# A graph, attention and mixture-of-experts layer: where the groups without edges stand, how the sorted places are loaded, and routed writes without a bound

## The chip, the cores and the metric

One of the cores of a Trainium2 chip runs the whole program in one launch. The metric is the device time of one execution in microseconds (us). The engines are PE (TensorE), DVE (VectorE), ACT (ScalarE), POOL (GpSimd) and SP (SyncE); the last two also issue transfers.

## The reference

```python
xn = _layernorm(x)                                   # x: 6250 x 256, 100000 edges (src, dst)
# graph attention over the edges, rows = src, neighbours = dst
e = leaky(f_dst_part[dst] + f_row_part[src] + a_b)   # slope 0.2
ex = exp(e - segment_max(e, src)[src])
h = relu(segment_sum(ex / denom[src] * Wh[dst], src))
# linear attention with 8 heads and a feed-forward block on xn, each with a layernorm
x = x + h + mix(xn)
# 6 experts of three 256x256 layers, the best two of each row by a router
x = x + moe(_layernorm(x))
```

## The kernel before

The 6250 nodes are 50 blocks (NT) of R = 125 rows. **Sorting.** The edges come sorted by dst and are needed by src, so the kernel sorts them on the chip: DVE and PE turn 28 chunks of edges into places, and POOL writes each chunk's words to `sorted_slots` in HBM (L524). An edge's place is in one of TILES = 812 tiles of L = 128; the tiles of a block follow those of the block before, and two blocks can share one. While the sorting runs, the linear attention is worked off between its steps in numbered slots (`attend`).

**The group table.** The graph loop takes the edges in groups of GT = 4 tiles, each of one block. How many groups a block needs depends on the data (`ngf`, from its first and last tile), but the loop has a fixed number, NG = 251, enough for any input. So DVE computes, from the counts, a word per group: its first tile `tf`, its place in the ring and its block (`group_tab`, one row of 251 words). Before the change the groups that are left over stand behind the last block's: `over` is held at block NT - 1 and `tf` at TILES - 4. To go from 50 blocks to 251 groups, PE multiplies 0/1 comparisons (`gcmp`) with a column per block. A second row of the table says, for each of NB = 203 ring places, how many groups must be done before the place is filled anew.

**Sorted places.** When the last chunk is written (`sent_runs`), SP loads the 812 x 128 words back as `raw`, in seven transfers of up to 128 tiles; PE transposes them (L1218) and DVE makes of them the index table of the gathers and the row table (L894 to L900). Then a barrier ends the block of code.

**The graph loop.** POOL gathers rows of `wh_table` (1036 bytes each) by an indirect transfer per tile (L1306) into a ring of RING = 11 places of four tiles, and waits for `room` before it fills a place again. SP watches what landed and counts `ready`; it also waits, for the place two ahead, until PE's `total` has freed it, and copies three tiles at each turn of the ring. Each group passes fixed stages, one slot apart, on all engines: `own_rows` on ACT (L1495), which waits for `ready` and is the first to touch a group; `mark` on DVE (four of L1340); `turn` on PE one slot later; peak, `spread`, `fetch`; the scores at lag 4; `own_weight` and `weigh` at lag 5; `total` on PE at lag 6 (L1607, L1619); `gather_up` on DVE at lag 7 (L1409), which adds the group into its block's row of `acc_mem`. In every ten slots one of the 25 chunks of the feed-forward block is worked off as well. `acc_mem`, 128 x 12900, lies over the sorting's tables (`raw` among them) and has to be zero before the first `gather_up`; one memset at the loop's start does that (L1315).

**Routing and experts.** The router works in five parts of 6, 10, 10, 12 and 12 tiles of rows. As soon as a part's places are known (`d_pos`, L1904) POOL writes every row twice, 125 rows of 264 words per indirect transfer (L1809): 12, 20, 20, 24 and 24 of them. Each has a bound, `bounds_check=last_row`. When all have landed the expert stage reads the rows back in tiles of 256, PE multiplies them three times, and POOL adds the results to the output (L2110).

## Time and profile before

| | |
|---|---|
| median of 3 runs | 2435.78 us (2430.62 to 2439.38) |
| the profiled execution | 2439.61 us |
| its span, first to last instruction | 2437.9 us |
| busy: PE, DVE, ACT, POOL | 1952.8, 1758.0, 1440.8, 1129.3 us |
| mean granted clock of PE | 0.915 of full speed |

Busy times are sums over stages that have different limits, so no share of the span says which engine matters; each stage is read by itself. A source view gives for one line of the code how often it ran, the least, median and greatest length of one in ns, and when the first and the last started. A bracket behind a row of the timeline tells how long the engine had been idle before it and whose event ended that; "issue" is time in which it waited for nothing that the profile shows.

### The profile page before, as it was taken

Reading aid. Unit: us, or ns where it says so; the run is one execution under the profiler, and the core shown is the slowest. Engines: PE = TensorE matmul, PEld = TensorE weight load, DVE = VectorE, ACT = ScalarE, POOL = GpSimd, SP = SyncE. Lnnn points to the kernel's source line nnn. Section 1 sums busy time; section 2 is a strip of 40 time slices with the busy share of each in tenths; the row PEclk is TensorE's granted clock in tenths of the full one; section 3 lists DMA queues with packets and bytes.
Section 4 is the critical chain, followed back from the end, with each engine's and each line's share of the span. In section 5 each row is a group of like instructions: output and inputs, shape, how many; then the busy total and the mean of one; then the engine's idle time right before and its main releaser. Section 6 shows DMA issues by size and latency. Waiting matters only on the chain. (4 is left out here: it accounts for less than half of the span.)

```text
span 2437.9 us, 50376 instructions
## 1 busy us (share of the span) xinstructions
PE 1952.8 (80%) x10273; PEld 1581.1 (65%) x10273; DVE 1758.0 (72%) x5447; ACT 1440.8 (59%) x4447; POOL 1129.3 (46%) x1089
## 2 busy tenths in 40 slices
PE   2888856598874888988889998998799564399997
PEld 1444435477762777767677877777678463288886
DVE  7877769999984778787768888887788752155543
ACT  3566547233311778877778888887688762133332
POOL 0000000011125777777777777777720177455555
PEclk9899967799986999999999999999999875699998
DMA  4200000011112444444444444444410455255553
GB/s 136 59 26 27 28 2 22 13 55 23 24 21 76 121 118 116 122 124 117 121 117 118 121 117 121 117 116 121 124 41 6 123 141 139 75 88 92 94 97 57
DMA packets 123284, 205.68 MB, mean 84 GB/s; under 512 B 34806, under 2 KB 77667, under 8 KB 122987
## 3 DMA queue, kind: packets, MB, share of 16 engines
q0 software_dynamic: 69648, 135.12, 23.8%
q1 hardware_dynamic: 48681, 59.88, 8.3%
q10 hardware_dynamic: 4658, 7.46, 1.1%
q8 instruction: 96, 1.57, 0.3%
q14 instruction: 201, 1.65, 0.2%
HBM read 146.67 MB, written 49.70 MB: 81 GB/s over the span
## 5 line engine op out<-in xcount | busy, mean ns | idle before, releaser
L1306 POOL DMA_INDIRECT area<-wh_table,area x812 | 783.8, 965 | 260.1 <-issue 246.4
L1619 PE MATMUL bank<-area 128*126 x2008 | 512.4, 399 | 103.8 <-ACT area L1542 70.1
L1619 PEld LDWEIGHTS bank<-area 128*126 128x126 f32 x2008 | 366.6, 192 | 186.8 <-issue 134.0
L1340 DVE TENSOR_SCALAR area<-iota_row,area 128x126 f32<-128x126 f32 x1004 | 357.9, 364 | 33.1 <-ACT area L1495 27.5
L1528 ACT ACTIVATE area<-iota_row,area 128x126 f32<-128x126 f32 x753 | 292.4, 389 | 0.4 <-ACT area L1535 0.3
L1409 DVE SCALAR_TENSOR_TENSOR acc_mem<-acc_mem,area,bank 125x258 f32 x251 | 120.7, 481 | 179.6 <-PE bank L1607 168.1
L1542 ACT ACTIVATE area<-area 128x126 f32<-128x126 f32 x753 | 243.1, 387 | 0.5
L2110 POOL DMA_INDIRECT out_dram<-area x108 | 169.2, 1567 | 158.7 <-DVE area L2171 142.3
L519 POOL IOTA acc_mem<- 50x812 f32 x1 | 0.8, 807 | 457.7 <-DVE area L789 457.7
L1481 ACT ACTIVATE area<-bank 125x512 bf16<-125x512 f32 x251 | 148.7, 592 | 95.8 <-DVE area L1350 94.0
L1639 PE MATMUL bank<-area 128*128 128x250 f32 x800 | 191.0, 382 | 4.0 <-ACT area L1555 4.0
L1650 PE MATMUL bank<-area 128*125 128x256 f32 x800 | 193.3, 385 | 0.0
L1595 PE MATMUL bank<-ident,area 128*126 128x128 f32 x1004 | 161.7, 284 | 35.3 <-DVE area L1340 34.9
L1639 PEld LDWEIGHTS bank<-area 128*128 128x128 f32 x800 | 156.3, 196 | 25.0 <-ACT area L1555 4.5
L1350 DVE TENSOR_REDUCE area<-bank 125x1 f32<-125x512 f32 x251 | 171.6, 684 | 0.0
L1650 PEld LDWEIGHTS bank<-area 128*125 128x125 f32 x800 | 153.7, 192 | 24.7
L1495 ACT ACTIVATE area<-area,iota_blk 128x4 f32 x251 | 74.5, 297 | 140.0 <-SPq L1298 122.7
L524 POOL DMA_INDIRECT sorted_slots<-area x28 | 46.0, 1645 | 230.4 <-DVE area L868 209.3
L2171 DVE SCALAR_TENSOR_TENSOR area<-bank,area 128x256 f32<-128x256 f32 x108 | 47.6, 480 | 144.2 <-DMA out_dram<-area 81.9
L1809 POOL DMA_INDIRECT moe_rows<-area x100 | 120.9, 1209 | 63.3 <-ACT area L1960 33.8
L1595 PEld LDWEIGHTS bank<-ident,area 128*126 128x126 f32 x1004 | 106.4, 141 | 39.8 <-DVE area L1340 39.4
L2203 ACT ACTIVATE area<-bank,area 128x256 f32<-128x256 f32 x108 | 45.3, 471 | 139.8 <-issue 133.6
(395 smaller groups left out, 4217.1 us busy)
## 6 DMA issues: line engine op xcount, KB each, us to landing
area<-moe_rows SPq DMA_DIRECT2D x54, 264.0 KB, 2.7
area<-wh_table,area POOLq DMA_INDIRECT x812
area<-area SPq DMA_DIRECT2D x18, 388.5 KB, 3.4
wh_table<-area SPq DMA_DIRECT2D x50, 126.5 KB
xn<-in_x_dram SPq DMA_DIRECT2D x25, 250.0 KB
x_rows<-area SPq DMA_DIRECT2D x25, 250.0 KB
area<-x_rows ACTq DMA_DIRECT2D x24, 250.0 KB
area<-in_L_ffn_expert_w_dram SPq DMA_DIRECT2D x3, 1536.0 KB, 12.1
```

The lines of the kernel that those rows point to most:

```text
L1306: g.indirect_dma_start(out=gath[:, (i + GT) % RS, :], out_offset=None, in_=table, in_offset=bass.IndirectOffsetOnAxis(ap=idx_tab[:, i:i + ...
L1340: ins = V.tensor_scalar(xm[:, b, t, :], iota_row[:, :], rowl[:, j % 10, t:t + 1], fetched(j, D)[:, t:t + 1], ALU.is_equal, ALU.mult)
L1350: V.tensor_reduce(gmax[0:R, b:b + 1], bank[XT[j % 2]][0:R, :], AX.X, ALU.max).then_inc(d_m, 1)
L1481: A.activation(hot[0:R, b, :], bank[XT[j % 2]][0:R, :], ACT.Sign).then_inc(a_hot, 1)
L1528: last = A.activation(dist[:, t, :], iota_row[:, :], ACT.Abs, bias=rowl[:, j % 10, t:t + 1], scale=-1.0)
L1542: last = A.activation(sm[:, b, t, :], dist[:, t, :], ACT.Exp, bias=e3[:, b, t:t + 1], scale=-1.0e12)
L1595: last = T.transpose(bank[XT[j % 2]][0:RW, t * L:(t + 1) * L], xm[:, b, t, :], ident[:, :])
L1619: last = T.matmul(bank[US[b]][0:RW, 0:WROW], sm[:, b, t, :], gath[:, bass.ds(place + t, 1), 0:WROW].rearrange("p a w -> p (a w)"), start=( ...
L1639: last = T.matmul(bank[HB[p % 2]][:, i * CH:(i + 1) * CH], w_1[:, k, f * 128:(f + 1) * 128], x1T[:, k, :], start=(k == 0), stop=(k == 1))
L1650: last = T.matmul(bank[AB][0:R, r * D:(r + 1) * D], hT[:, f, r * R:(r + 1) * R], w_2[:, f, :], start=(f == 0), stop=(f == 7))
L1809: g_.indirect_dma_start(out=moe_rows, out_offset=bass.IndirectOffsetOnAxis(ap=posi3[0:R, b, k, i:i + 1], axis=0), in_=pay3[0:R, b, i, :], ...
L2110: g.indirect_dma_start(out=out, out_offset=bass.IndirectOffsetOnAxis(ap=rowi[:, j % RB6, s, MW - 2:MW - 1], axis=0), in_=yo[:, j % 3, s, : ...
```

## The change

Three edits. First, the left-over groups are shared out: after block b, `sparef` = (b + 1) x left / 50 + 0.25 as an integer have been laid, and each belongs to an extra block 50, whose rows in `acc_mem`, `own_mem` and `fr_c` nobody reads, and begins at the tile that the next block's first group begins with. Two comparisons are needed (`gcmp`, `gspare`), four matmuls of 251 columns, and a turn of `tf` by PE for the second row of the table. The memset of `acc_mem` is split: the columns that the sorting doesn't use (5360) are cleared ahead of the wait for the transposes, the others (7798) by `clear`, lag 3, in the loop's fourth slot. Second, `raw` is loaded by two transfers. Third, L1809 has no bound.

```diff
-        own_mem = sb("own_mem", [R, NT * 3 * (1 + OLD)])
+        own_mem = sb("own_mem", [R, (NT + 1) * 3 * (1 + OLD)])
-        acc_mem = sb("acc_mem", [128, NT * WROW])
-        acc = acc_mem[0:R, :].rearrange("p (b w) -> p b w", w=WROW)
+        acc_mem = sb("acc_mem", [128, (NT + 1) * WROW])
+        acc_all = acc_mem[0:R, :].rearrange("p (b w) -> p b w", w=WROW)
+        acc = acc_all[:, 0:NT, :]
...
                 sp.wait_ge(sent_runs, 16 * KC)
-                for i in range(-(-TILES // 128)):
-                    n = min(128, TILES - i * 128)
-                    sp.dma_start(raw[0:n, i, :], slots[i * 128 * L:(i * 128 + n) * L].rearrange("(t l) -> t l", l=L)).then_inc(slots_in, 16)
+                full = TILES // 128
+                sp.dma_start(raw[:, 0:full, :], slots[0:full * 128 * L].rearrange("(i t l) -> t i l", t=128, l=L)).then_inc(slots_in, 16)
+                sp.dma_start(raw[0:TILES - full * 128, full, :],
+                             slots[full * 128 * L:TILES * L].rearrange("(t l) -> t l", l=L)).then_inc(slots_in, 16)
...
                 step(V.tensor_copy(ngf, int50))
+                V.tensor_tensor(packed[:, 3, :], firstf[:, 1:NT + 1], firstf[:, 0:NT], ALU.subtract)
                 step(V.tensor_tensor_scan(gend, ones[:, 0:NT], ngf, 0.0, ALU.mult, ALU.add))
...
+                V.tensor_copy(packed[:, 5, :], tmp50)
+                step(V.tensor_scalar(left, gend[:, NT - 1:NT], -1.0, float(NG), ALU.mult, ALU.add))
+                V.tensor_copy(packed[:, 4, :], firstf[:, 1:NT + 1])
+                step(V.tensor_scalar(lastf, iota_g[:, 1:NT + 1], left, 1.0 / NT, ALU.mult, ALU.mult))
+                step(V.tensor_scalar(int50, lastf, 0.25, None, ALU.add))
+                step(V.tensor_copy(sparef[:, 1:NT + 1], int50))
+                V.tensor_tensor(packed[:, 0, :], gend, sparef[:, 1:NT + 1], ALU.add)
+                step(V.tensor_tensor(ngf, ngf, sparef[:, 1:NT + 1], ALU.add))
+                V.tensor_tensor(packed[:, 1, :], gend, sparef[:, 0:NT], ALU.add)
+                step(V.tensor_tensor(packed[:, 2, :], ngf, sparef[:, 0:NT], ALU.subtract))
+                step(V.tensor_tensor(packed, packed, ident[:, 0:NT].unsqueeze(1).to_broadcast([128, 6, NT]), ALU.mult))
+                step(V.tensor_reduce(cols, packed, AX.X, ALU.add))
+                V.tensor_scalar(gspare, iota_g[0:NT, :], rcol[0:NT, :], None, ALU.is_ge)
                 V.tensor_scalar(gcmp, iota_g[0:NT, :], gcol[0:NT, :], None, ALU.is_ge).then_inc(gcmp_ready, 1)
...
                 dve.wait_ge(gmap_done, 1)
-                step(V.scalar_tensor_tensor(tf, iota_g, float(GT), bank[KV][:, 128:128 + NG], ALU.mult, ALU.add))
-                V.tensor_scalar(over, bank[KV + 1][0:1, 128:128 + NG], float(NT - 1), None, ALU.min)
...
+                begun, ended = bank[KV][0:1, 0:NG], bank[KV + 1][0:1, 0:NG]
+                groups, past = bank[KV][0:1, 256:256 + NG], bank[KV + 1][0:1, 256:256 + NG]
+                step(V.tensor_copy(whole, ended))
+                V.tensor_tensor(shown, iota_g[0:1, :], groups, ALU.subtract)
+                step(V.tensor_tensor(spot, past, whole, ALU.subtract))
+                V.tensor_scalar(over, whole, -1.0, float(NT), ALU.mult, ALU.add)
+                step(V.scalar_tensor_tensor(shown, spot, -1.0, shown, ALU.add, ALU.mult))
+                V.tensor_tensor(over, spot, over, ALU.mult)
+                step(V.scalar_tensor_tensor(tf, shown, -float(GT), begun, ALU.mult, ALU.add))
+                V.tensor_tensor(over, over, whole, ALU.add)
+                V.tensor_scalar(tf, tf, float(TILES - GT), None, ALU.min).then_inc(gcmp_ready, 1)
+                dve.wait_ge(gcmp_ready, 2)
...
+                dve.wait_ge(gmap_done, 2)
+                V.tensor_scalar(tq0, bank[KV][:, 508:509], -3.0, 1.0 / GT, ALU.add, ALU.mult)
...
+                V.memset(acc_mem[:, ZERO_FROM:], 0.0)
                 dve.wait_ge(tab_pe, 1)
...
-                T.matmul(bank[KV][:, 128:128 + NG], more[0:NT, :], gcmp, start=True, stop=True)
-                T.matmul(bank[KV + 1][:, 400:401], gcmp[:, 0:L], wcol[0:NT, :], start=True, stop=True)
-                T.matmul(bank[KV + 1][0:NG - L, 401:402], gcmp[:, L:NG], wcol[0:NT, :], start=True, stop=True)
-                T.matmul(bank[KV + 1][:, 128:128 + NG], ones[0:NT, :], gcmp, start=True, stop=True).then_inc(gmap_done, 1)
+                T.matmul(bank[KV][0:1, 0:NG], dcolf[0:NT, :], gspare, start=True, stop=True)
+                T.matmul(bank[KV][0:1, 256:256 + NG], scol[0:NT, :], gcmp, start=True, stop=True)
+                T.matmul(bank[KV + 1][0:1, 0:NG], ones[0:NT, 0:1], gcmp, start=True, stop=True)
+                T.matmul(bank[KV + 1][0:1, 256:256 + NG], ones[0:NT, 0:1], gspare, start=True, stop=True).then_inc(gmap_done, 1)
+                pe.wait_ge(gcmp_ready, 2)
+                T.matmul(bank[KV][:, 508:509], tf[:, 0:L], ones[0:1, 0:1], start=True, stop=True)
+                T.matmul(bank[KV][0:NG - L, 509:510], tf[:, L:NG], ones[0:1, 0:1], start=True, stop=True).then_inc(gmap_done, 1)
...
-                V.memset(acc_mem[:, :], 0.0).then_inc(acc_zero, 1)
-                dve.wait_ge(acc_zero, 3)
+                dve.wait_ge(acc_zero, 2)
...
+                def clear(s, j):
+                    if at(s) == 0:
+                        V.memset(acc_mem[:, 0:ZERO_FROM], 0.0).then_inc(acc_zero, 1)
...
-                               (4, score_less_max)], feed)
+                               (4, score_less_max), (3, clear)], feed)
...
                             g_.indirect_dma_start(out=moe_rows, out_offset=bass.IndirectOffsetOnAxis(ap=posi3[0:R, b, k, i:i + 1], axis=0),
-                                                  in_=pay3[0:R, b, i, :], in_offset=None,
-                                                  bounds_check=last_row, oob_is_err=False).then_inc(sent[b], 16)
+                                                  in_=pay3[0:R, b, i, :], in_offset=None).then_inc(sent[b], 16)
```

The order of the instructions, in two places. On DVE, where the group table is made (`bank` is PSUM; 1x251 is one row over the groups). Before:

```order
L822 SCALAR_TENSOR_TENSOR acc_mem<-area,bank 128x251 [waits gmap_done]
L823 TENSOR_SCALAR acc_mem<-bank 1x251 [waits rank_step]
L824 SCALAR_TENSOR_TENSOR acc_mem<-area,bank 128x1
L825 SCALAR_TENSOR_TENSOR acc_mem<-area,bank 123x1
L826 TENSOR_SCALAR acc_mem<-acc_mem 128x251
L827 TENSOR_SCALAR acc_mem<-acc_mem 128x1 [waits rank_step]
L828 TENSOR_SCALAR acc_mem<-acc_mem 123x1
L829 SCALAR_TENSOR_TENSOR acc_mem<-acc_mem 1x251
L830 TENSOR_SCALAR acc_mem<-acc_mem 128x1 [waits rank_step]
```

and in the change, behind the same wait for PE:

```order
L837 COPY acc_mem<-bank 1x251 [waits gmap_done]
L838 TENSOR_TENSOR acc_mem<-area,bank 1x251 [waits rank_step]
L839 TENSOR_TENSOR acc_mem<-bank,acc_mem 1x251
L840 TENSOR_SCALAR acc_mem<-acc_mem 1x251 [waits rank_step]
L841 SCALAR_TENSOR_TENSOR acc_mem<-acc_mem 1x251
L842 TENSOR_TENSOR acc_mem<-acc_mem 1x251 [waits rank_step]
L843 SCALAR_TENSOR_TENSOR acc_mem<-acc_mem,bank 1x251
L844 TENSOR_TENSOR acc_mem<-acc_mem 1x251 [waits rank_step]
L845 TENSOR_SCALAR acc_mem<-acc_mem 1x251
L847 SCALAR_TENSOR_TENSOR acc_mem<-acc_mem 1x251 [waits gcmp_ready]
L848 TENSOR_SCALAR acc_mem<-acc_mem 1x251 [waits rank_step]
```

Operations on single columns (128x1, 123x1) gave way to ones on rows of 251, and the second wait for PE stands further down, ahead of the comparisons for the ring. On DVE, at the end of the sorting, behind the last `join` (L868 before, L887 now). Before:

```order
L868 SCALAR_TENSOR_TENSOR area<-area,bank 106x64 [waits sent_runs,halved] x2
L894 CAST acc_mem<-bank 128x512 [waits tab_pe]
L894 CAST acc_mem<-bank 128x300
L896 TENSOR_SCALAR area<-acc_mem 128x812 [waits rank_step]
L897 TENSOR_SCALAR acc_mem<-acc_mem 128x812
```

and in the change:

```order
L887 SCALAR_TENSOR_TENSOR area<-area,bank 106x64 [waits sent_runs,halved] x2
L910 MEMSET acc_mem 128x5360
L914 CAST acc_mem<-bank 128x512 [waits tab_pe]
L914 CAST acc_mem<-bank 128x300
L916 TENSOR_SCALAR area<-acc_mem 128x812 [waits rank_step]
```

A memset of 5360 columns now stands ahead of the wait for `tab_pe`, the transposes. On DVE, in the graph loop, between the last two marks of group 3 (ISA rows fetch a register) and the next slot, which begins with `group_peak`. Before:

```order
L1331 ISA
L1340 TENSOR_SCALAR area<-iota_row,area 128x126
L1331 ISA
L1340 TENSOR_SCALAR area<-iota_row,area 128x126
L1350 TENSOR_REDUCE area<-bank 125x1 [waits p_xt]
L1262 TENSOR_LOAD group_tab
```

and in the change:

```order
L1353 ISA
L1362 TENSOR_SCALAR area<-iota_row,area 128x126
L1353 ISA
L1362 TENSOR_SCALAR area<-iota_row,area 128x126
L1371 MEMSET acc_mem 128x7798
L1376 TENSOR_REDUCE area<-bank 125x1 [waits p_xt]
L1285 TENSOR_LOAD group_tab
```

The memset that stood at the loop's start (L1315, 12900 columns) is gone from there, and 7798 columns of it stand here.

## Rows read from the trace of the kernel before

**Rows 1.** Windows: us, busy us (count) of each engine, clock, DMA.

```profile
core 0: us, PE busy (x) PEld busy (x) DVE busy (x) ACT busy (x) POOL busy (x), PEclk, DMA share, GB/s
...
480.00:733.00 253.00, 215.85 (x1424) 190.66 (x1424) 231.16 (x376) 74.67 (x197) 42.95 (x26) 0.92 0.13 29
...
754.80:1787.50 1032.70, 896.39 (x5053) 744.62 (x5054) 808.61 (x3133) 802.95 (x2897) 783.80 (x812) 0.96 0.43 119
1787.50:1893.00 105.50, 100.17 (x589) 83.92 (x587) 87.79 (x350) 92.80 (x334) 0.00 (x0) 1.00 0.02 7
```

**Rows 2.** Source view of the gathers, L1306 (ns; first and last start us).

```profile
L1306 POOL DMA_INDIRECT area<-wh_table,area x812: 949/949/1543, 754.9 to 1785.1; - x163
```

**Rows 3.** Source view of own_rows, L1495, one per group; what ended idleness.

```profile
L1495 ACT ACTIVATE area<-area,iota_blk x251: 282/297/302, 761.6 to 1891.8; 128x4 f32 x126
...
  SPq L1298: 122.7, 61
```

**Rows 4.** The same line, window 1278 to 1474 us.

```profile
L1495 ACT ACTIVATE area<-area,iota_blk x48: 291/298/300, 1278.6 to 1473.0; 128x4 f32 x48
```

**Rows 5.** The same line, window 1787.5 to 1893 us.

```profile
L1495 ACT ACTIVATE area<-area,iota_blk x26: 291/297/298, 1788.0 to 1891.8; 128x4 f32 x26
```

**Rows 6.** Source view of gather_up, L1409, one per group.

```profile
L1409 DVE SCALAR_TENSOR_TENSOR acc_mem<-acc_mem,area,bank x251: 467/483/485, 798.7 to 1914.1; 125x258 f32 x126
```

**Rows 7.** Timeline, POOL: start us, length us, line; near 815 us.

```profile
815.27 0.95 POOL L1306 DMA_INDIRECT area<-wh_table,area  x1 [0.30 <-issue]
```

**Rows 8.** Timeline, DVE, start of the graph stage.

```profile
757.28 10.81 DVE L1315 MEMSET acc_mem<- 128x12900 f32 x1 [2.62 <-issue]
```

**Rows 9.** Timeline, DVE, where the group table is made.

```profile
467.24 0.26 DVE L803 TENSOR_TENSOR_SCAN acc_mem<-ones,acc_mem 128x50 f32<-128x50 f32 x1
...
470.09 0.25 DVE L817 TENSOR_TENSOR own_mem<-own_mem 125x50 f32<-125x50 f32 x1
...
472.85 0.42 DVE L822 SCALAR_TENSOR_TENSOR acc_mem<-area,bank 128x251 f32<-128x251 f32 x1 [0.36 <-PE bank L1197]
...
479.34 0.64 DVE L872 MEMSET area<- 128x308 uint32 x2
```

**Rows 10.** Timeline, PE, the first of the four matmuls for it.

```profile
469.93 1.20 PE L1194 MATMUL bank<-area 50*128 50x251 f32 x2 [5.68 <-DVE area L815]
```

**Rows 11.** Timeline, SP, PE weight load and DVE, 744 to 751 us.

```profile
744.31 3.14 SPq L476 DMA_DIRECT2D acc_mem<-sorted_slots  x7
748.79 1.14 PEld L1218 LDWEIGHTS bank<-ident,acc_mem 128*128 128x128 f32 x6 [10.69 <-DMA acc_mem<-sorted_slots]
...
750.64 1.07 DVE L894 CAST acc_mem<-bank 128x512 int32<-128x512 f32 x2 [17.57 <-PE bank L1218]
```

**Rows 12.** The page, DMA issues: KB each, us from issue to landing.

```profile
area<-area SPq DMA_DIRECT2D x18, 388.5 KB, 3.4
```

**Rows 13.** Source view of the routed writes, L1809.

```profile
L1809 POOL DMA_INDIRECT moe_rows<-area x100: 1185/1194/1623, 1942.9 to 2100.6; - x100
```

**Rows 14.** Timeline, POOL, at the starts of the second and fourth bursts.

```profile
1968.35 1.34 POOL L1809 DMA_INDIRECT moe_rows<-area  x1 [7.06 <-ACT area L1960]
...
2029.91 1.21 POOL L1809 DMA_INDIRECT moe_rows<-area  x1 [0.30 <-POOL area L1802]
```

**Rows 15.** Timeline, DVE, L1904, which lets bursts three and four start.

```profile
1991.36 0.18 DVE L1904 CAST area<-area 125x20 int32<-125x20 f32 x1
...
2020.41 0.18 DVE L1904 CAST area<-area 125x24 int32<-125x24 f32 x1
```

**Rows 16.** Source view of the sorting writes, L524.

```profile
L524 POOL DMA_INDIRECT sorted_slots<-area x28: 1547/1550/3732, 507.9 to 740.6; - x28
```

**Rows 17.** Source view of the output writes, L2110.

```profile
L2110 POOL DMA_INDIRECT out_dram<-area x108: 1544/1554/1774, 2129.8 to 2428.1; - x108
```

**Rows 18.** The page, part 5, one kind of VectorE instruction.

```profile
L1340 DVE TENSOR_SCALAR area<-iota_row,area 128x126 f32<-128x126 f32 x1004 | 357.9, 364 | 33.1 <-ACT area L1495 27.5
```

More of the change, by code:

```diff
@@ L248, in gps_kernel @@
         iota_g, gcmp = take(NG), take(NG)[0:NT, :]
-        more = take(128)
         rstd_all, nmr = (take(NT)[0:R] for _ in range(2))
@@ L322, in gps_kernel @@
         int50, end50 = (a.bitcast(I32) for a in smallt[7:9])
-        firstf = take(NT + 1)
-        gcol, csrc, tcol, wcol, pcol, tq0, tq1 = (take(1) for _ in range(7))
+        firstf, sparef = take(NT + 1), take(NT + 1)
+        csrc, left, tq0, tq1 = (take(1) for _ in range(4))
+        cols = take(6)
+        gcol, rcol, scol, dcolf, tcol, pcol = (cols[:, i:i + 1] for i in range(6))
         srci, dsti = wpos.bitcast(I32), bpos.bitcast(I32)
@@ L335, in gps_kernel @@
         behind = take(L)[0:NT, :]
-        tf = take(NG)
+        tf = take(NG)[0:1, :]
         spot, whole, over = (take(NG)[0:1, :] for _ in range(3))
@@ L340, in gps_kernel @@
         rcmp = take(2, NB)
+        gspare = take(NG)[0:NT, :]
+        shown = take(NG)[0:1, :]
+        packed = take(6, NT)
+        ZERO_FROM = take.place[0]
         XB, QB, HEADS, NUM, DEN, OUT = 0, 1, 2, 3, 4, 5
@@ L801, in _ @@
                 V.memset(firstf[:, NT:NT + 1], float(TILES))
+                V.memset(sparef[:, 0:1], 0.0)
                 step(V.tensor_copy(ngf, int50))
+                V.tensor_tensor(packed[:, 3, :], firstf[:, 1:NT + 1], firstf[:, 0:NT], ALU.subtract)
                 step(V.tensor_tensor_scan(gend, ones[:, 0:NT], ngf, 0.0, ALU.mult, ALU.add))
-                step(V.scalar_tensor_tensor(ngf, ngf, -float(GT), firstf[:, 1:NT + 1], ALU.mult, ALU.add))
-                V.tensor_tensor(tmp50, tmp50, ident[:, 0:NT], ALU.mult)
@@ L813, in _ @@
-                step(V.tensor_reduce(gcol, tmp50, AX.X, ALU.add))
-                V.tensor_scalar(more[0:NT, :], ones[0:NT, :], wcol[0:NT, :], None, ALU.mult)
-                V.tensor_scalar(gcmp, iota_g[0:NT, :], gcol[0:NT, :], None, ALU.is_ge).then_inc(gcmp_ready, 1)
-                step(V.tensor_scalar(own_all[:, :, 0, 0], frd, csrc[0:R, :], None, ALU.add))
-                step(V.tensor_tensor(own_all[:, :, 0, 1], own_all[:, :, 0, 0], own_bits[:, :, 0, 0], ALU.subtract))
-                V.tensor_tensor(own_all[:, :, 0, 2], own_all[:, :, 0, 1], own_bits[:, :, 0, 1], ALU.subtract)
@@ new lines, in _ @@
+                step(V.tensor_reduce(cols, packed, AX.X, ALU.add))
+                V.tensor_scalar(gspare, iota_g[0:NT, :], rcol[0:NT, :], None, ALU.is_ge)
+                V.tensor_scalar(gcmp, iota_g[0:NT, :], gcol[0:NT, :], None, ALU.is_ge).then_inc(gcmp_ready, 1)
+                V.memset(own_all[:, NT:NT + 1, 0, :], 0.0)
+                V.memset(fr_c[:, NT:NT + 1], 0.0)
+                step(V.tensor_scalar(own_all[:, 0:NT, 0, 0], frd, csrc[0:R, :], None, ALU.add))
+                step(V.tensor_tensor(own_all[:, 0:NT, 0, 1], own_all[:, 0:NT, 0, 0], own_bits[:, 0:NT, 0, 0], ALU.subtract))
@@ L829, in _ @@
-                step(V.scalar_tensor_tensor(word, over, 65536.0, tf[0:1, :], ALU.mult, ALU.add))
-                V.tensor_scalar(tq0, tq0, 1.0 / GT, None, ALU.mult)
-                step(V.tensor_scalar(tq1[0:NG - L, :], tq1[0:NG - L, :], -3.0, 1.0 / GT, ALU.add, ALU.mult))
-                V.tensor_scalar(rcmp[:, 0, :], iota_g[:, 0:NB], tq0, None, ALU.is_ge)
-                V.tensor_scalar(rcmp[0:NG - L, 1, :], iota_g[0:NG - L, 0:NB], tq1[0:NG - L, :], None, ALU.is_ge).then_inc(gcmp_ready, 1)
@@ L834, in _ @@
-                step(V.tensor_scalar(spot, tf[0:1, :], float(GT), None, ALU.add))
+                begun, ended = bank[KV][0:1, 0:NG], bank[KV + 1][0:1, 0:NG]
[4 more added lines that the diff above has]
+                V.tensor_scalar(over, whole, -1.0, float(NT), ALU.mult, ALU.add)
@@ new lines, in _ @@
+                step(V.scalar_tensor_tensor(shown, spot, -1.0, shown, ALU.add, ALU.mult))
[4 more added lines that the diff above has]
+                dve.wait_ge(gcmp_ready, 2)
+                step(V.scalar_tensor_tensor(word, over, 65536.0, tf, ALU.mult, ALU.add))
@@ L835, in _ @@
+                step(V.tensor_scalar(spot, tf, float(GT), None, ALU.add))
                 step(V.tensor_scalar(turns, spot, 0.5, 1.0 / RS, ALU.add, ALU.mult))
@@ L883, in _ @@
                     if k == 2:
[L884 removed]
+                        dve.wait_ge(gmap_done, 3)
                         dve.wait_ge(halved, 1)
@@ L1233, in gps_kernel @@
         pair = take(GT, 2)
-        peak = take(NT)
+        peak = take(NT + 1)
         e1, e2, e3 = (take(2, GT) for _ in range(3))
@@ L1322, in block_of @@
                 def block_of(j):
-                    return dve.snap(blocks[j % 10], min_val=0, max_val=NT - 1)
+                    return dve.snap(blocks[j % 10], min_val=0, max_val=NT)
                 def load_place(s, j):
@@ L1497, in block_of @@
                 def block_of(j):
-                    return act.snap(blocks[j % 5], min_val=0, max_val=NT - 1)
+                    return act.snap(blocks[j % 5], min_val=0, max_val=NT)
                 def rescale(s, j):
@@ L1602, in fetch @@
                     wait(pe, d_es, at(s, 3, -5))
-                    r = pe.snap(blocks[b], min_val=0, max_val=NT - 1)
+                    r = pe.snap(blocks[b], min_val=0, max_val=NT)
                     g = 1 + at(s) % OLD
```

40 lines of the change are left out of this document (16 added, 24 removed).

## Prediction, made before the changed kernel was run

> **What bounds the kernel now.** The windows view gives the stages [rows 1]. From 754.8 to 1787.5 us all five engines work at the graph loop: POOL gathers 812 tiles of 128 table rows, and PE, DVE and ACT work them off in groups of four. From 1787.5 to 1893 POOL is idle and the others go on at full pace. The source view of the gathers says why: first start 754.9, last 1785.1 [rows 2], so 1030.2/811 = 1.270 us per gather and 5.08 per ring place of four. Busy is 0.949 of it; with the bare issue gap a gather costs 1.25, so the queue never pauses for long. On the other side stands `own_rows`, once per group, from 761.6 to 1891.8, and 122.7 us of ACT's idle time before it ended with SP's word that tiles have landed, in 61 places [rows 3]. So the loop is bound by gathers until 1787 and by the group pipeline after it.
>
> What a group costs when nothing is missing is read from two stretches: (1473.0 - 1278.6)/47 = 4.136 us while gathers run [rows 4] and (1891.8 - 1788.0)/25 = 4.152 after they ended [rows 5]. They agree, so the gathers don't slow the engines; I take 4.15. The 25 groups behind the last gather are the kernel's empty ones. Counting the reference's edge list by the kernel's rule gives blocks of 4 (24 of them) or 5 (26) groups, 226 with edges, of 251. Before, the 226 are paced by the gathers, though 1030/4.15 = 248 would fit, and then the 25 are paid alone: 104 us with POOL idle.
>
> The second POOL-bound stretch is the routing: 100 writes of L1809 [rows 13], the second burst starting at 1968.35 [rows 14] and the last write at 2100.6, at 1.50 us each. Then nothing else is left of that stage, and the expert stage, bound by PE, can't start before they land.
>
> **Part 1, empty groups between the blocks.** Half a group per block is laid behind it; none is left at the end. The engines then need 251 x 4.15 = 1042 us for what POOL feeds in 1030: engines and gathers are level, the engines a little behind. The start is still fed by POOL. Group 13, counted from 0, reads tiles 47 to 50, in ring place 12; that place's first gather starts at 815.27 [rows 7], its fourth 3.8 later, and from there to `own_rows` takes 2.9 (1785.1 to 1788.0) [rows 2, 5]: 822.0. From there 237 groups x 4.15 = 983.6, so the last `own_rows` stands at 1805.6. I add 4 us for places where groups still wait, such as the ring wrap. 1809.6 against 1891.8 [rows 3]: **-82**. What follows it stays: the last `gather_up` comes 22 us later [rows 6].
>
> Bounds: it can't end before its tiles, 1788.0, which is -104. Above: a ring place is freed when `total` of its groups is done. At the start `own_rows` to `gather_up` takes 798.7 - 761.6 = 37 us [rows 3, 6], at the end 22; call it 32 with full feed. 11 places are 56 us of gathers, less 32, less 7 for gather and landing: 17 us, four groups, that the engines may fall behind before POOL is held. The longest run of 5-group blocks has nine; with half an empty group each takes 22.8 us and feeds on 16.1 tiles, 20.5: +2.3 a block, +21 in the run. So POOL is held some 4 to 10 us there, while the engines stay busy; in a run of 4-group blocks they catch up and may wait for the tiles that came late. If each held us is lost and other runs add as much, -62. I keep -82.
>
> The table that places them costs DVE more. Before, from the scan to L817 are 14 steps in 2.85 us [rows 9], 0.20 each; now 19 steps, two of them on 300 columns (+0.25 each): +1.5. PE multiplies four times 251 columns instead of twice; a pair of passes takes 1.20 [rows 10], two small ones go: +1.2 of waiting for DVE. From L822 to L872 DVE took 6.5 us [rows 9]; six more operations of one row by 251, some 0.33, four single columns of 0.1 less: +1.6. Together **+4**. It isn't hidden: DVE is busy 231 of the 253 us behind it [rows 1], and each step of the sorting waits for it. Bounds +2 (half swallowed by the waits there) and +6. The new second wait, for `tf` turned by PE, stands behind seven operations of DVE and costs nothing; PE holds its `inverses` for it by some 4 us, of which DVE wants the result 10 us later.
>
> The clearing of `acc_mem` was one memset of 10.81 us at 757.28 [rows 8]. Now 5360 columns (4.5 us at that rate) lie in DVE's wait of 17.57 us for the transposes [rows 11]: nothing. The other 7798 (6.5 us) stand in slot 3 of the loop, near 777 us, where a group comes only each 5.02 us. Up to group 13 DVE has 45 us for ten groups, and a group costs it 87.8/25 = 3.5 us [rows 1]: 35 + 6.5 fit, so nothing; at worst 3, if all engines need 4.15 (41.5 + 6.5). While the old memset ran, gathers went on at 1.25 us. The Trainium skill, page "SBUF — State Buffer", section "SBUF: two separate sides", says that a VectorE operation in a two-port mode locks GpSimd out, so that its DMAs lack descriptors. By that rule, were a memset such an operation, the 6.5 us would be added to the gathers and the total be 2342 to 2343; the row speaks against it.
>
> **Part 2, two transfers for seven.** SP's seven issues take 3.14 us from 744.31, PE starts at 748.79, 4.5 behind the first [rows 11]. A transfer of 388.5 KB, nearly the new one's 384, lands 3.4 us after its issue [rows 12]: 747.7, with the small one and PE's start 748. **-1**; bounds 0 and -2.
>
> **Part 3, writes without a bound.** Two kinds of rows bear on it. The gathers have no bound and take 0.949 + 0.303 = 1.252 [rows 2]; the routed writes, with one, 1.194 + 0.303 = 1.497 [rows 13]. If the difference is the bound, each saves 0.245. But the sorting writes (106 rows of 64) have none either and take 1.55 [rows 16], as the output writes with bound and addition do [rows 17]: shape and direction count as well. The gather is nearest in width (259 and 264 columns, 128 and 125 rows), so I take 0.245; ends are 0 and +0.36 more per write. The second burst starts with DVE, so 88 writes are on the path: -21.6. Bursts two and three end 40 x 0.245 = 9.8 earlier than 2029.91 [rows 14], at 2020.1, and burst four needs L1904 of 2020.41 [rows 15]: 0.7 is lost. **-21**.
>
> **Sum.** The profiled execution took 2439.6 us (span 2437.9 and 1.7 around it), 3.8 over the median. 2439.6 + 4 - 1 - 82 - 21 = 2339.6; less 3.8: **2336**.
>
> **Rivals.** A, as above, 0.50. B, the bound costs nothing and the 0.245 is the scatter's or the 125 rows': 2336 + 21 = 2357; speaks for it that the sorting writes are dear without one; 0.22. C, the bare writes cost like those, 1.55: 88 x 0.36 = 32 more than before, 2389; 0.05. D, POOL and engines hold each other by turns, -62: 2356; for it speaks that both sides are within 2% of each other with 17 us between them; 0.12. E, DVE locks POOL: if each of the 25 added groups' five operations of 0.364 [rows 18] stopped the gathers for its length, 45 us, the gathers end at 1834 instead of 1788 and own 250 with them, some 26 above my 1809.6: 2362. That is the port rule named above as a mechanism here; the mean step of 5.08 against the bare 5.01 leaves 14 us for all such stops in 226 groups, 1.6 for 25 more; 0.03. F, the empty groups stay at the end because of how the shares are rounded: 2439.6 + 3 - 21 - 3.8 = 2418; the shares come in steps of half a group, so little speaks for it; 0.03. G, slower: the empty groups close the ring on itself. A place's way round (gather and landing 7, own to total 32, release some 2, and up to two empty groups more, 8) is 49 us for 11 places of 5.08, 56. Beyond 56 the loop goes by the way, not by the engines, and since the loop takes 1137 us now (754.9 to 1891.8) and the other parts give 18, it passes the old time from (1137 + 18)/203 x 11 = 63 us. If it were 66, 203 x 6 = 1218, 81 over: 2336 + 82 + 81 = 2499; 0.03.
>
> Range: A alone 2323 to 2348. With B, D and most of E 2318 to 2368, leaving C, F, G and the tails out. A measurement here tells some 0.3% (7 us) from no change. Faster holds A to F, 0.95; slower G and the worst of C, 0.03; same 0.02.
>
> **What would show it.** `own_rows` without a long stretch behind the last gather: last gather near 1795, last `own_rows` near 1813 (with the +3), steps of 4.15 throughout, ACT's waits for SP below 30 us; POOL's waits for room some 5 to 25 us where before they were 0.9. If the step in the loop is above 4.3, or both waits stand at 40 us, the -82 is wrong. L1904's copies at the same distances, L1809's successor with a median of 0.95; at 1.19 B holds, at 1.55 C. The first gather at 758; PE's transposes 3.7 behind SP's first issue. DVE from the scan to the first one-hot 4 us longer.

## The result, and the profile after

The changed kernel took 2350.3 us (median of 4, 2348.6 to 2353.0), the kernel before in the same session 2436.8; the ratio is 0.965, 95% interval 0.963 to 0.967. So 86.5 us were won, where 100 were forecast. Executions in a slower state are left out of a ratio, so it can differ a little from the quotient of the two medians.

The windows view of the kernel after, with the columns of [rows 1]:

```profile
core 0: us, PE busy (x) PEld busy (x) DVE busy (x) ACT busy (x) POOL busy (x), PEclk, DMA share, GB/s
480.00:731.00 251.00, 213.38 (x1426) 188.72 (x1427) 231.52 (x377) 74.69 (x197) 42.83 (x26) 0.94 0.13 30
750.80:1791.00 1040.20, 962.53 (x5581) 805.35 (x5582) 882.36 (x3452) 892.87 (x3202) 782.61 (x811) 0.98 0.43 118
1791.00:1800.00 9.00, 9.00 (x56) 7.61 (x55) 7.01 (x31) 7.20 (x27) 0.95 (x1) 1.00 0.12 32
```

The stretch of 105 us in which POOL had nothing left [rows 1] is 9 us now. The stretch before it is only 7.5 us longer, and DVE and ACT do 319 and 305 more instructions in it: the empty groups' work. The source views of the gathers, of `own_rows` and of `gather_up`, as in [rows 2, 3, 6]:

```profile
L1329 POOL DMA_INDIRECT area<-wh_table,area x812: 945/947/1519, 750.8 to 1791.1; - x163
its engine sat idle before it (us, times) until:
  issue: 241.6, 793
  SPq L1316: 16.0, 18
```

```profile
L1523 ACT ACTIVATE area<-area,iota_blk x251: 283/297/301, 758.4 to 1799.5; 128x4 f32 x126
its engine sat idle before it (us, times) until:
  SPq L1321: 27.7, 9
```

```profile
L1437 DVE SCALAR_TENSOR_TENSOR acc_mem<-acc_mem,area,bank x251: 466/482/485, 793.7 to 1821.8; 125x258 f32 x126
```

First to last `own_rows` is 1041.1 us; before it was 1130.2 [rows 3]. ACT waits for tiles in 9 places instead of 61, and 22.9 of the 27.7 us stand before the first five groups, where the gathers have only begun. POOL now waits for room in the ring (SP's L1316) in 18. The timeline of POOL between 1395 and 1450 us, its rows that ended such a wait:

```profile
1398.99 0.94 POOL L1329 DMA_INDIRECT area<-wh_table,area  x1 [4.86 <-SPq L1316]
...
1420.12 0.94 POOL L1329 DMA_INDIRECT area<-wh_table,area  x1 [1.11 <-SPq L1316]
...
1444.91 0.94 POOL L1329 DMA_INDIRECT area<-wh_table,area  x1 [4.46 <-SPq L1316]
```

They fall where the engines are at the end of the run of nine blocks with five groups each and just behind it, 10.4 of the 16.0 us. The source view of the routed writes, to be set against [rows 13], shows the part that failed:

```profile
L1836 POOL DMA_INDIRECT moe_rows<-area x100: 1174/1180/1500, 1852.0 to 2009.3; - x100
```

A median of 1.180 us without the bound, 1.194 with it; first to last write 157.3 us, before 157.7. The timeline of POOL, SP, PE's weight load and DVE between the sorting and the loop, beside [rows 8, 11]:

```profile
737.23 1.54 POOL L531 DMA_INDIRECT sorted_slots<-area  x1 [3.61 <-DMA sorted_slots<-area]
...
740.95 0.38 SPq L481 DMA_DIRECT2D acc_mem<-sorted_slots  x1
...
741.38 0.48 SPq L482 DMA_DIRECT2D acc_mem<-sorted_slots  x1
...
744.69 1.15 PEld L1241 LDWEIGHTS bank<-ident,acc_mem 128*128 128x128 f32 x6 [10.30 <-DMA acc_mem<-sorted_slots]
...
746.54 1.07 DVE L914 CAST acc_mem<-bank 128x512 int32<-128x512 f32 x2 [11.58 <-PE bank L1241]
...
750.78 1.00 POOL L1329 DMA_INDIRECT area<-wh_table,area  x1 [12.01 <-POOLq L449]
```

The transposes stand 3.74 us behind SP's first issue (before 4.48). The part of the memset that moved into the loop, in DVE's timeline:

```profile
776.66 6.56 DVE L1371 MEMSET acc_mem<- 128x7798 f32 x1 [1.57 <-PE bank L1623]
```

DVE's row of the new table, from the scan on (before: [rows 9]):

```profile
463.59 0.25 DVE L812 TENSOR_TENSOR_SCAN acc_mem<-ones,acc_mem 128x50 f32<-128x50 f32 x1
...
467.57 0.25 DVE L830 TENSOR_TENSOR own_mem<-own_mem 125x50 f32<-125x50 f32 x1
...
470.93 0.41 DVE L837 COPY acc_mem<-bank 1x251 f32<-1x251 f32 x1 [0.95 <-PE bank L1217]
...
476.90 0.41 DVE L854 SCALAR_TENSOR_TENSOR group_tab<-acc_mem 1x251 int32<-1x251 f32 x1
```

### The profile page after: what moved, and what is told of

It is laid out like the page before. It is cut to its first block and busy times, and to the rows that moved or that the text cites. A ratio compares the mean times of both kernels' runs of the same rounds, so it can differ in the third digit from the quotient of the medians.

```text
span 2346.8 us, 50388 instructions
## 1 busy us (share of the span) xinstructions
PE 1927.8 (82%) x10277; PEld 1565.0 (67%) x10277; DVE 1758.4 (75%) x5456; ACT 1446.5 (62%) x4447; POOL 1128.2 (48%) x1089
## 5 line engine op out<-in xcount | busy, mean ns | idle before, releaser
L1647 PE MATMUL bank<-area 128*126 x2008 | 497.5, 390 | 34.4 <-ACT area L1570 15.7
L1647 PEld LDWEIGHTS bank<-area 128*126 128x126 f32 x2008 | 358.6, 188 | 110.1 <-issue 58.4
L1678 PEld LDWEIGHTS bank<-area 128*125 128x125 f32 x800 | 150.1, 188 | 22.9
L1205 PE MATMUL bank<-area 128*128 128x128 f16 x784 | 104.6, 298 | 7.5 <-DVE area L887 7.5
```

What stands on the lines that cost most here:

```text
L1647: last = T.matmul(bank[US[b]][0:RW, 0:WROW], sm[:, b, t, :], gath[:, bass.ds(place + t, 1), 0:WROW].rearrange("p a w -> p (a w)"), start=( ...
L1678: last = T.matmul(bank[AB][0:R, r * D:(r + 1) * D], hT[:, f, r * R:(r + 1) * R], w_2[:, f, :], start=(f == 0), stop=(f == 7))
```

## The experiments

The first four kernels shared a chip with runs of the kernel before (2435.2 us there, median of 19).

**e1_nobound**: the kernel before, with the bound alone taken from the routed writes.

```diff
-                last_row = g_.to_reg(ROWS - 1)
...
-                                                   in_=pay3[0:R, b, i, :], in_offset=None,
-                                                   bounds_check=last_row, oob_is_err=False).then_inc(sent[b], 16)
+                                                   in_=pay3[0:R, b, i, :], in_offset=None).then_inc(sent[b], 16)
```

> The kernel before with one edit: the routed writes have no bound. Theory (the bound is nearly free, read from the changed kernel's write median of 1.181 us against 1.194): the hundred writes take 100 x 0.013 = 1 us less, the time is 2436 within its spread. Rival (the bound costs 0.245 a write, and in the changed kernel something else, such as the graph stage ending earlier, took the gain back): 2436 - 21 = 2415.

Measured: 2434.8 us, ratio 1.000 (0.9986 to 1.0013). The source view of its routed writes:

```profile
L1808 POOL DMA_INDIRECT moe_rows<-area x100: 1174/1179/1489, 1935.4 to 2091.6; - x100
```

First to last write is 156.2 us. Against the median of 1.194 with the bound [rows 13] a write is 0.015 us shorter, and the theory that the bound costs 0.245 falls. First to last `own_rows` is 1126.2 us here, 4 less than in the profiled execution of the kernel before (1130.2), though the loop is the same: so much can lie between two single executions.

**e3_groups**: the changed kernel with the bound and the seven loads put back, so that the groups, their table and the split memset are left.

```diff
-                full = TILES // 128
-                sp.dma_start(raw[:, 0:full, :], slots[0:full * 128 * L].rearrange("(i t l) -> t i l", t=128, l=L)).then_inc(slots_in, 16)
-                sp.dma_start(raw[0:TILES - full * 128, full, :],
-                             slots[full * 128 * L:TILES * L].rearrange("(t l) -> t l", l=L)).then_inc(slots_in, 16)
+                for i in range(-(-TILES // 128)):
+                    n = min(128, TILES - i * 128)
+                    sp.dma_start(raw[0:n, i, :], slots[i * 128 * L:(i * 128 + n) * L].rearrange("(t l) -> t l", l=L)).then_inc(slots_in, 16)
...
+                                                   bounds_check=last_row, oob_is_err=False).then_inc(sent[b], 16)
```

> The changed kernel with the routed writes' bound and the seven loads put back, so that only the groups without edges and the split memset are left of the change. Theory: they are the whole gain but for 1 us of the loads and 1 of the writes, so 2350 + 2 = 2352. Rival (the parts help each other, or the other two parts bring more than they show): 2360 or more.

Measured: 2349.5 us (2345.9 to 2355.2), ratio 0.966 (0.964 to 0.969): all of the gain within the noise (2352 was expected). First to last `own_rows` is 1039.9 us. From the last sorting write to the transposes it takes 8.20 us, as before; with two loads 7.47.

**e4_at_end**: the changed kernel with every block's share made zero, so that all empty groups stand at the end again and the rest of the change stays.

```diff
-                step(V.tensor_scalar(int50, lastf, 0.25, None, ALU.add))
+                step(V.tensor_scalar(int50, lastf, 0.0, None, ALU.mult))
```

> The changed kernel with the shares set to zero: all its operations for the table run, but every group without edges stands at the end again, with the extra block as its block. Theory (the placing alone brings the gain): the loop from first to last own_rows goes back from 1041 to about 1130 us, the total to 2350 + 89 = 2439 minus nothing, so 2436 to 2440. Rival (the memset moved off the start, or another edit, brings part of the 89): below 2430. It also prices the table: against before it has the table's cost of 4 and the loads' and writes' 2 of gain.

Measured: 2429.9 us (2426.4 to 2439.7), ratio 0.999 (0.998 to 1.001). Source view of `own_rows` in it:

```profile
L1523 ACT ACTIVATE area<-area,iota_blk x251: 282/297/301, 761.2 to 1886.4; 128x4 f32 x126
its engine sat idle before it (us, times) until:
  SPq L1321: 105.3, 47
```

1125.2 us from first to last, with ACT's waits for tiles back at 105 us. With the same table, loads, writes and memsets the gain is gone: it is the place of the empty groups. The time lies below the 2436 to 2440 expected and just under the rival's 2430, which gave another edit part of the gain. It doesn't speak for that rival: the interval of the ratio holds 1, the loop is only 1.0 us shorter than in e1_nobound, which has none of these edits, and the four times of the changed kernel, which differs from this one in that one line, all lie 73 us or more below the lowest here (2426.4).

**e7_prices**: a kernel of its own that leaves the whole computation out and returns zeros. POOL issues twelve indirect transfers of one kind back to back, waits for them, then the next kind, and all twice: rows of 264 numbers, 128 or 125 of them, read, written, and written under a bound; and rows of 64 numbers written 106, 112 and 128 at a time.

> A small kernel of its own, without the computation: POOL issues twelve indirect transfers of each kind back to back, twice: gathers of 128 and of 125 rows by 264 words, writes of 125 and 128 rows with and without a bound, writes of 106, 112 and 128 rows by 64 words. Theory 1 (the number of rows sets POOL's time, by how it divides among the queues): 125 rows cost about 1.19 as gather and as write, with or without a bound, 128 rows about 0.95, and 106 rows 1.55. Theory 2 (the direction does): all gathers near 0.95, all wide writes near 1.19, narrow ones 1.55. Theory 3 (the bound does): 1.19 with and 0.95 without.

Its groups by line (L60 read 128 rows, L64 read 125, L68 write 125 with the bound, L72 without, L76 write 128 with it, L80 without):

```profile
L68 POOL DMA_INDIRECT write_bound<-src,idx x24 | 28.8, 1198 | 14.4 <-DMA got<-gather,idx 7.7 <-issue 6.7
L64 POOL DMA_INDIRECT got<-gather,idx x24 | 28.6, 1194 | 14.1 <-DMA got<-gather,idx 7.4 <-issue 6.7
L72 POOL DMA_INDIRECT write<-src,idx x24 | 28.3, 1180 | 24.3 <-issue 13.6 <-DMA write_bound<-src,idx 10.7
L76 POOL DMA_INDIRECT write_bound<-src,idx x24 | 23.7, 989 | 12.7 <-issue 6.7 <-DMA write<-src,idx 5.9
L80 POOL DMA_INDIRECT write<-src,idx x24 | 23.3, 970 | 10.2 <-issue 6.7 <-DMA write_bound<-src,idx 3.5
L60 POOL DMA_INDIRECT got<-gather,idx x24 | 22.9, 955 | 35.6 <-DMA gather<-src 27.4 <-issue 6.7 <-DMA write_narrow<-src,idx_n 1.4
```

And from POOL's timeline the first of twelve with 106, 112 and 128 short rows:

```profile
153.51 1.56 POOL L86 DMA_INDIRECT write_narrow<-src,idx_n  x1 [1.77 <-DMA write<-src,idx]
...
177.96 0.94 POOL L86 DMA_INDIRECT write_narrow<-src,idx_n  x1 [2.48 <-DMA write_narrow<-src,idx_n]
...
193.96 0.98 POOL L86 DMA_INDIRECT write_narrow<-src,idx_n  x1 [1.43 <-DMA write_narrow<-src,idx_n]
```

The bound adds 0.018 to 0.019 us and the direction 0.015 at most. What counts is the number of rows: 125 cost 1.18 to 1.20 us, 128 cost 0.955 to 0.99, 112 cost 0.94 and 106, fewer than any, 1.56. The Trainium skill, page "DMA: Bandwidth & Descriptors", section "Why a DMA increments its semaphore by 16 and not by 1", states that a transfer runs on the largest number of DMA engines up to 16 that divides the slowest dimension of both its sides, with an exception for some direct copies. Where that dimension is the rows, as here, this makes 16 for 128 and 112, 5 for 125 and 2 for 106. The trace agrees: by its DMA records a transfer of 125 wide rows goes in thirty packets of four rows and five of one, which is five shares of 25; one of 106 short rows in six packets of 16 rows and two of 5, two shares of 53; 112 and 128 short rows in 16 packets of 7 and of 8.

The section gives no time on POOL. In these rows it grows with the length of one share: 7 rows 0.94 us, 8 rows 0.97, 25 rows 1.18, 53 rows 1.55, as a rough estimate from these four 0.013 us for each row of a share. Nothing here shows what POOL does in that time.

**e5_ng247, e6_ring10, e8_even, e9_clear** went to another chip, on which the kernel before itself took 2798.4 us (median of 35 runs) instead of 2435. In the order of their names they are: four empty groups fewer (which also leaves out the last steps of the last feed-forward chunk); ten ring places instead of eleven; shares by the running count of tiles; the memset whole again.

> The changed kernel with 247 groups instead of 251: 21 without edges instead of 25 (enough for these edges, not for any). Theory (the loop is now bound by the group pipeline): each group taken away saves 4.15 us while the gathers' end, some 1791, allows it: from the last own_rows at 1799.5 it can fall by about 8 to 10 before the tiles of the last group hold it, so 6 to 12 us of the 16.6. Rival A (bound by the pipeline throughout, gathers far from mattering): -16.6. Rival B (already bound by the gathers): 0 to -2.

> The changed kernel with a ring of 10 places instead of 11. Theory (the ring's slack covers the runs of full blocks: 17 us at 11 places, 12 at 10): POOL is held for room some 5 us more in each of the long runs, so 20 to 50 us in all instead of 16, and since the engines stay busy meanwhile, the time grows by 0 to 8 us. Rival (both sides hold each other by turns, so the slack decides): the time grows by 15 or more.

> The changed kernel with the groups without edges placed so that the running count of groups follows the running count of tiles (none behind blocks of five groups, one behind most of four) instead of half a group each. Two more small operations in the table, 0.6 us. Theory (what is left above the engines' pace are waits at the start, which no placing mends, and POOL's holds in runs of full blocks, 16 us, which cost the engines nothing while they are busy): POOL's holds fall to near 0 and the time stays within 3 us of 2350. Rival (the holds come back as waits): 8 or more faster.

> The changed kernel with the clearing of the accumulators in one memset at the loop's start again. Theory (DVE has time up to group 13, where the tiles set the pace): 0 to 4 us slower. Rival (since the engines are the bound now and the start is behind, the 10.8 us add in full): 8 to 11 slower.

Measured: 2794.4, 2801.8, 2794.1 and 2811.5 us, ratios to the kernel before 0.997, 0.999, 1.000 and 1.004, with half-widths of 0.003 to 0.004; one of the ten executions of e9_clear took 6585.5 us. All four expectations were worked out for 2350 us, so none of these runs says what its edit does, and the change's whole gain is missing in all four. In e8_even every other stage has its usual length within 2 us; the groups take 1479.8 us from first to last. The view of waits over the whole execution, e8_even, from its first lines (us in total, times, longest; lines stand two below those of the change):

```profile
POOL area L1331 <- SPq L1318: 478.1, 155, 15.9
...
ACT area L1511 <- DVE area L1378: 354.4, 129, 8.6
DVE acc_mem L1439 <- remote: 337.9, 62, 8.8
PEld bank L1637 <- issue: 271.8, 89, 25.7
```

and the timeline of e8_even for PE's `fetch` (L1637) and `total` (L1649) and DVE's `gather_up` (L1439), which waits for both:

```profile
1015.46 0.25 PE L1637 MATMUL bank<-own_mem,area 125*128 x4
...
1016.04 1.91 PE L1649 MATMUL bank<-area 128*126 x8
...
1022.95 0.48 DVE L1439 SCALAR_TENSOR_TENSOR acc_mem<-acc_mem,area,bank 125x258 f32 x1 [8.23 <-remote]
```

The matmuls stand in the record at 1015.5 and 1016 to 1018, but the trace's semaphore events show `fetch`'s count rise at 1022.62 and `total`'s at 1022.77. In the kernel after on the ordinary chip the count rises 0.01 us behind `fetch`'s last matmul, and more than 1 us behind it once in 251 groups; here that is so 86 times. DVE, ACT and SP all wait for those counts, and through SP so does POOL. The ends of matmuls in a record are modelled, so it stays open whether the matmuls ended late or only their counts came late, and why on that chip was not found.

Why the gain is missing there can be argued from the same trace. The source view of `own_rows`:

```profile
L1525 ACT ACTIVATE area<-area,iota_blk x251: 288/298/302, 758.1 to 2237.9; 128x4 f32 x126
...
  SPq L1323: 10.6, 5
```

From the fourteenth on a group takes 5.83 us, more than the 5.08 in which POOL's gathers filled a ring place before. So ACT waits for tiles in 5 places only, while POOL waits for room in 155. There are no waits for tiles that an empty group could fill, all 251 groups are paid at the groups' pace wherever the empty ones stand, and a ratio of 1.00 is what that gives. It is not shown for the kernel before itself, which was not profiled on that chip.

The last four went together to a third chip, with the kernel before at 2435.0 us. **r_after** is the changed kernel unaltered:

> The changed kernel unaltered, beside the other three of this call on one chip, since four variants went to a chip on which the kernel before took 2798 us and told nothing there. Theory that the second chip is the exception: on an ordinary chip before is 2430 to 2440 us and this 2346 to 2354, ratio 0.965. Rival, that the change's gain depends on the chip: before near 2800 again, and this within 0.5% of it, with TensorE's completions of the fetch products up to 7 us after their records in a third of the groups.

Measured: 2347.5 us (2344.8 to 2348.2), ratio 0.963 (0.961 to 0.965). The ordinary result came back; the second chip is the exception of the three. e5_ng247 was not repeated, so what an empty group less would bring on an ordinary chip is not shown.

**e10_even**: the same kernel as e8_even.

```diff
-                step(V.tensor_scalar(lastf, iota_g[:, 1:NT + 1], left, 1.0 / NT, ALU.mult, ALU.mult))
-                step(V.tensor_scalar(int50, lastf, 0.25, None, ALU.add))
+                step(V.scalar_tensor_tensor(lastf, firstf[:, 1:NT + 1], NG / TILES, gend, ALU.mult, ALU.subtract))
+                step(V.tensor_scalar(lastf, lastf, left, 0.0, ALU.min, ALU.max))
+                step(V.tensor_tensor_scan(tmp50, ones[:, 0:NT], lastf, 0.0, ALU.mult, ALU.max))
+                step(V.tensor_scalar(int50, tmp50, 0.25, None, ALU.add))
```

> The empty groups laid by the running count of tiles instead of the running number of the block: a block gets its share when the groups so far fall behind 249/812 of the tiles so far. Theory that POOL's gathers set the pace after the change (5.13 us a place of which 5.02 are the four gathers) and its 16.0 us of waits for room are all that even placing can give back: POOL waits for room 0 to 8 us, the loop 5 to 16 us shorter than 1041.0 us, 2335 to 2346 us in all on an ordinary chip. Rival, that the groups' own pace of 4.135 us sets it and the holds lie beside it: loop and time unchanged within 3 us, though the room waits fall. On a chip where before takes 2798: no difference to it, as seen once.

Measured: 2346.4 us (2345.0 to 2348.6), 1.1 under r_after, ranges overlapping. Source views of the gathers and of `own_rows`, and from the view of waits POOL's for room:

```profile
L1331 POOL DMA_INDIRECT area<-wh_table,area x812: 946/949/1542, 750.6 to 1778.2; - x163
```

```profile
L1525 ACT ACTIVATE area<-area,iota_blk x251: 288/297/302, 757.9 to 1796.6; 128x4 f32 x126
```

```profile
POOL area L1331 <- SPq L1318: 1.2, 4, 0.3
```

POOL's waits for room fall from 17.7 us (r_after) to 1.2, and its gathers take 12.0 us less (1027.6 against 1039.6). The groups take 1038.7 against 1040.6, at 4.137 us a group from the fourteenth on against 4.134. So the theory that POOL's gathers set the pace after the change falls: the groups' own pace does, and POOL's holds lie beside it.

**e11_ring10**: `RING = 10` for 11, the same kernel as e6_ring10.

> Ten places of gathered tiles in flight instead of eleven. Theory that the ring is nearly closed on itself (eleven places at 5.13 us are 56 us of way round, and POOL already stands 16.0 us for room in the run of blocks with five groups): every hold grows by up to the 5.0 us of one place, room waits 40 to 100 us, 2365 to 2410 us. Rival, that the ring has slack outside that run: room waits 20 to 30 us and 2350 to 2358 us. On a chip where before takes 2798: no difference to it, as seen once.

Measured: 2356.2 us (2352.6 to 2357.6), 8.7 above r_after. POOL's waits for room are 25.5 us in 21 places, ACT's for tiles 35.8 in 16, a group costs 4.159 us and the loop is 4.1 longer. The 40 to 100 us of the first theory are not there, so the ring has slack outside the run of nine blocks. Of the profiled execution's 9.4 us over r_after's, 3.5 stand in the sorting, which the edit doesn't touch (more on that at the end); the cost of the place itself is measured by the loop, 4 us between one profiled execution of each.

**e12_clear**: one memset at the loop's start, the same kernel as e9_clear.

```diff
-                V.memset(acc_mem[:, ZERO_FROM:], 0.0)
...
+                V.memset(acc_mem[:, :], 0.0).then_inc(acc_zero, 1)
...
-                               (4, score_less_max), (3, clear)], feed)
+                               (4, score_less_max)], feed)
```

> The whole zeroing of the sums (13,158 numbers in each partition, 11 us) put back to the loop's start, in place of 5,360 numbers before the loop and 7,798 beside the first gathers. Theory that the zeroing lies beside the first gathers either way: first own_rows unchanged within 1 us and the time within 4 us of the changed kernel's. Rival, that the first sum waits for it: first own_rows the same, first gather_up later by 3 to 5 us, and the time 3 to 5 us above the changed kernel's on an ordinary chip.

Measured: 2343.8 us (2341.1 to 2353.2), ratio to the kernel before 0.963; 3.7 under r_after, but with ranges that overlap widely. Timeline of its DVE and POOL at the loop's start:

```profile
750.01 11.02 DVE L1337 MEMSET acc_mem<- 128x13158 f32 x1 [2.67 <-issue]
```

```profile
751.37 0.95 POOL L1328 DMA_INDIRECT area<-wh_table,area  x1 [0.30 <-issue]
...
760.14 0.95 POOL L1328 DMA_INDIRECT area<-wh_table,area  x1 [0.30 <-issue]
```

Gathers go on at 1.253 us beside a VectorE memset of 11 us ((760.14 - 751.37)/7). First `own_rows` to first `gather_up` takes 32.2 us, with the split memset 35.7 (r_after): the part in the loop does hold up the first sum by 3.5, and the loop as a whole is 1.2 us shorter without it (1039.5 against 1040.6). The rival, that the whole memset holds the first sum up, falls with its sign reversed.

## Why the prediction came out as it did

The time was right within its range and the sign and the cause of the gain were right; the sum was 14 us too good, and the median lies 2 us above what rival A alone allowed. Some 5 of them are only how the profiled executions stand to their medians, 3.8 above before and 1.7 below after. The other 9 are looked for here, term by term, against the profiled executions (span 2437.9 before, 2346.8 after, so -91.1 where -100 was forecast):

**Empty groups between the blocks, -82 forecast.** The mechanism is as forecast, and e3_groups and e4_at_end show it from both sides. Measured from the first gather, the last `own_rows` was expected 1054.7 us later (1809.6 - 754.9) and came 1048.7 later, so the term is -88, or -84 against the loop of e1_nobound. Group 13 came at 68.6 instead of 67.1; 237 groups took 980.1 instead of 983.6 (4.135 each, the value of [rows 4], where 4.15 was taken); and the allowance of 4 us for places that still wait was not needed. POOL is held at the nine-block run, as worked out: 10.4 us in all, just above the 4 to 10. That none of it reaches the end, which the prediction only chose, e10_even shows: it takes those holds away and the loop gains 2 us at most. Rival D, engines and POOL holding each other by turns, and rival F with the groups at the end, fall; so does rival E, by which the gathers would have ended near 1834 and not at 1791.1, and rival G, by which the time would have risen.

**The table, +4.** From `dest` to the first one-hot 19.16 us, before and in e1_nobound 15.40: +3.8.

**Two loads, -1.** From the last sorting write to the transposes 7.47 us against 8.20: -0.7.

**The clearing, nothing.** Right for the end within what can be measured. But the reason given, that DVE has room for it until group 13, was too simple: the first sum is 3.5 us later, and the next groups catch that up. The rule of the Trainium skill that the prediction weighed (page "SBUF — State Buffer", section "SBUF: two separate sides": a VectorE operation in a two-port mode locks GpSimd out) would have lengthened the gathers beside the memset, were that such an operation. The trace shows nothing of it: 1.253 us a gather beside the memset is the bare step.

**Writes without a bound, -21.** This is the step that failed, by nearly the whole distance. The prediction took the difference between gather and routed write (0.949 against 1.194) for the price of the bound and named the other readings, direction and the 125 rows, only as rival B, 0.22. By e1_nobound and the kernel after the bound is 0.014 to 0.015 us; by e7_prices 0.21 to 0.24 is the row count of 125 instead of 128, and the bound and the direction are below 0.02 each. The prediction had a row that spoke for it, the sorting writes of 106 rows at 1.55 [rows 16], and put them aside because the gather was "nearest in width". Rival B's 2357 is nearest as a mechanism; the median came 7 lower, 6 of it by the loop term.

**What no term held.** The steps on which the edits have no bearing differ between the two profiled executions: everything ahead of `dest` -3.8, the sorting -3.4, from the last `own_rows` to the first routed write +1.3, the rest +0.3: -5.6 in all. With +20.7 for the writes, -6.1 for the groups and +0.1 for the two small terms that makes 9.1, the 9 us between -100 and -91. Part of this is luck: `dest` alone stands anywhere from 457.3 to 464.5 us in the profiled executions, whatever the edits, so the 5.6 that made up for a quarter of the miss on the writes could as well have been added to it.

The chance for faster, 0.95, rested on a stretch of 104 us with an idle engine. It was read rightly, but on one chip four variants of the change showed no gain at all; such a case had no line among the rivals. The stretch is worth something only where the gathers ahead of it are slower than the groups, 5.08 against 4.15 us here.

## What to carry to other kernels

Work without input, such as padding groups, belongs where the engines would otherwise wait for the producer; look for a stretch at the end in which the producer is idle and the consumers run at full pace, and for the consumer's wait count before it. It pays only where the producer is the slower side in the main: on the chip with 5.83 us a group it gave nothing. When two rows differ in several ways at once, the difference is no price of any one of them: here shape, direction and bound differed together, and a kernel with nothing but the transfers took them apart in one run. Once the waits for tiles are gone, the pace is that of the group pipeline (4.13 us), and levelling the producer further gives nothing. Which engine sets that pace was not tested; PE is the busiest, 962.5 of 1040.2 us.

## What was not expected of the hardware

An indirect transfer of 125 rows costs POOL 0.21 to 0.24 us more than one of 128, and one of 106 rows 0.6 more than one of 112. Writing 128 rows with three spare ones would, as an estimate from L72 and L80 of e7_prices, give 88 x 0.21 = 18 us where the bound gave nothing; that was not tried.

One chip of three took 2798 us for the kernel before, 15% more, and variants of the change 19% more, which their traces show in the loop. In e8_even the count for `fetch` came late, mostly by 2 to 8 us, in a third of the groups. No run shows the cause.

The sorting stage, from the first one-hot to the last sorting write, has two lengths in the thirteen profiled executions of the kernel and its variants: 257.0 to 257.3 us in five, on three chips, and 260.0 to 261.4 in eight. The same kernel had 257.2 as e8_even and 260.0 as e10_even, so the edits don't decide it; a difference of 3 us between single profiled executions of this kernel is not evidence.
